# Expert results of a graph and mixture layer added into the output tensor itself, with the copy from a scratch tensor left out

## The reference, cut to what matters

```python
xn = _layernorm(x)
x = x + gnn(xn, edges) + linear_attention(xn)      # first residual; the result is called x2 below
x = x + ffn(_layernorm(x))                         # second residual

def ffn(x):                                        # 8 experts, hidden width 384
    gate = x @ Wg + bg
    scores, idx = top_k(gate, 2)                   # two experts for each row
    h = gelu(x @ W1[e] + b1[e])                    # for each expert e
    y = h @ W2[e] + b2[e]
    return sum over the two chosen e of score * y
```

## Time and profile before

| what | value |
|---|---|
| median of three runs | 1122.59 us |
| the profiled execution's own time | 1124.31 us |
| its span, first to last instruction | 1122.6 us |
| mean granted clock of TensorE | 0.932 of full speed |
| PE busy | 977.9 us, 87% of the span |
| DVE busy | 760.7 us, 68% |
| ACT busy | 332.5 us, 30% |
| POOL busy | 117.2 us, 10% |
| DMA queue of SyncE and ScalarE plain transfers (q1) | 49514 packets, 116.25 MB |
| DMA queue of GpSimd's indirect transfers (q0) | 6048 packets, 21.24 MB |

### The profile page before, as it was taken

The page is one execution under the profiler, slowest core; times in us unless marked ns, Lnnn a source line. Parts: engine busy times, 40 slices in busy tenths (PEclk is TensorE's granted clock), DMA queues, the critical chain, the costliest instruction groups (busy, mean ns, idle before and its releaser), DMA issues.

```text
span 1122.6 us, 17243 instructions
## 1 busy us (share of the span) xinstructions
PE 977.9 (87%) x6460; PEld 708.2 (63%) x6460; DVE 760.7 (68%) x1704; ACT 332.5 (30%) x402; POOL 117.2 (10%) x123
## 2 busy tenths in 40 slices
PE   3799999999789979989988988969887399999991
PEld 2677776765454445545678988858865366666660
DVE  6576788877875686986587898599979823332221
ACT  3561122112004332522333333215335232222220
POOL 3000000000001000000000000000631123333321
PEclk9789999999989999999989999969898599999996
DMA  7350121134341826637687100006056545556546
GB/s 237 105 167 29 57 86 58 57 128 176 107 178 35 297 87 233 185 101 251 225 318 298 47 1 1 1 0 254 5 186 227 209 103 102 109 112 113 110 59 166
DMA packets 58521, 146.44 MB, mean 130 GB/s; under 512 B 11386, under 2 KB 30732, under 8 KB 55434
## 3 DMA queue, kind: packets, MB, share of 16 engines
q1 hardware_dynamic: 49514, 116.25, 29.6%
q0 software_dynamic: 6048, 21.24, 10.0%
q10 hardware_dynamic: 2880, 7.87, 1.8%
HBM read 95.94 MB, written 53.23 MB: 133 GB/s over the span
## 4 chain that ended last, share of the span: by engine, by line
PE 66%; DVE 21%; issue 4%; DMA 4%; ACT 3%; SPq 1%; DVEq 0%; POOLq 0%; ACTq 0%
PE PS L1733 39%; PE PS L1982 12%; DVE arena L1449 3%; PE PS L1809 3%; DVE arena L1455 3%; DVE arena L1493 3%; PE PS L2133 2%; PE PS L1789 1%; PE PS L1820 1%; PE PS L1824 1%; DVE arena L1465 1%; DMA arena<-in_L_gnn_W_dram 1%; DVE arena L1355 1%; DVE arena L1205 1%; DMA arena<-as_d 1%
## 5 line engine op out<-in xcount | busy, mean ns | idle before, releaser
L1733 PE MATMUL PS<-arena 128*128 128x384 f16 (+7 forms) x3396 | 573.0, 322 | 4.6 <-DVE arena L1719 1.9
L1733 PEld LDWEIGHTS PS<-arena 128*128 128x128 f16 (+2 forms) x3396 | 321.0, 99 | 214.8 <-issue 12.2
L1982 PE MATMUL PS<-arena 128*128 128x193 f32 (+1 forms) x1200 | 191.3, 323 | 21.7 <-DVE arena L1455 16.3
L1982 PEld LDWEIGHTS PS<-arena 128*128 128x128 f32 x1200 | 186.7, 200 | 26.3 <-DVE arena L1455 16.0
L1020 ACT ACTIVATE arena<-arena,AS 128x1280 f32<-128x1280 f32 x60 | 81.8, 1363 | 134.0 <-DVE arena L1449 133.8
L1723 DVE TENSOR_SCALAR arena<-PS,arena 128x768 f32<-128x768 f32 x27 | 27.5, 1018 | 138.1 <-PE PS L2159 138.1
L1449 DVE SCALAR_TENSOR_TENSOR arena<-arena,AS 128x1280 f32<-128x1280 f32 x60 | 94.4, 1576 | 0.0
L1455 DVE SCALAR_TENSOR_TENSOR arena<-arena 128x1280 f32<-128x1280 f32 x60 | 90.8, 1513 | 2.5 <-PE PS L1982 2.4
L1257 DVE TENSOR_SCALAR arena<-arena 128x240 f16<-128x240 f16 x324 | 90.0, 278 | 0.0
L1256 DVE TENSOR_SCALAR arena<-arena 128x128 f16<-128x128 f16 x324 | 81.1, 250 | 0.1
L1087 ACT ACTIVATE arena<-PS 128x1536 f16<-128x1536 f16 x27 | 39.2, 1451 | 100.3 <-PE PS L2133 100.3
(11 more groups left out here) (274 smaller groups left out, 953.1 us busy)
## 6 DMA issues: line engine op xcount, KB each, us to landing
arena<-in_L_ffn_W_dram SPq DMA_DIRECT2D x48, 384.0 KB, 4.1
fr_d<-arena SPq DMA_DIRECT2D x48, 384.0 KB, 3.3
arena<-fr_d SPq DMA_DIRECT2D x16, 1152.0 KB, 14.4
arena<-in_x_dram SPq DMA_DIRECT2D x18, 384.0 KB, 5.7
arena<-rr_d SPq DMA_DIRECT2D x4, 1280.0 KB, 8.3
acc_d<-arena SPq DMA_DIRECT2D x11, 384.0 KB, 2.6
g_d<-arena SPq DMA_DIRECT2D x10, 388.0 KB, 2.3
acc_d<-arena ACTq DMA_DIRECT2D x10, 384.0 KB, 2.3
```

What stands on the lines that cost most here:

```text
L1733: m = T.matmul(out, left[i][x], right[i][y], start=first and i + r == 0, stop=last and 3 * i + r == n - 1)
L1982: m = T.matmul(ps[b][:, r * (C + 1):(r + 1) * (C + 1)], PT[i % deep][:, d * P:(d + 1) * P], feats, start=t == 0 and r == 0, stop=t == NT - ...
```

## The change

The stores of x2 go to the output tensor `out` in place of `acc_d`, and the indirect adds go to `out` too. The last tile's store writes its 98 real rows only. The adds get a bound, N - 1 = 1249: an index above it is left out and is no error. So the results of empty slots (numbers from 1280 on) and of the 30 padding rows (1250 to 1279) are written nowhere. The final DMA from `acc_d` to `out` and the wait on it are gone, as are the tile of zeros written to the end of `acc_d` and its share in two waits. `acc_d` still carries the sums of the first residual.

```diff
@@ line 292
-        acc_d = nc.dram_tensor("acc_d", (NP + P, D), F32, kind="Internal").ap()
+        acc_d = nc.dram_tensor("acc_d", (NP, D), F32, kind="Internal").ap()
@@ SyncE, line 583
-            sp.dma_start(acc_d[NP:NP + P, :], zrow).then_inc(s_xs_blank, 16)
@@ SyncE, the end, line 739
-            sp.dma_start(out, acc_d[0:N, :]).then_inc(s_out_done, 16)
-            sp.wait_ge(s_out_done, 16)
@@ GpSimd, line 847
-            pool.wait_ge(s_xs_blank, 32)
+            pool.wait_ge(s_xs_blank, 16)
@@ GpSimd, sums_add, line 858
-                g.indirect_dma_start(out=acc_d, out_offset=bass.IndirectOffsetOnAxis(ap=found[:, i:i + 1].bitcast(U32), axis=0),
-                                     in_=Yb[:, i % 2, :], in_offset=None, compute_op=ALU.add).then_inc(sums_out[i % 2], 16)
+                g.indirect_dma_start(out=out, out_offset=bass.IndirectOffsetOnAxis(ap=found[:, i:i + 1].bitcast(U32), axis=0),
+                                     in_=Yb[:, i % 2, :], in_offset=None, compute_op=ALU.add, bounds_check=N - 1, oob_is_err=False).then_inc(sums_out[i % 2], 16)
@@ ScalarE, line 972
-            act.wait_ge(s_xs_blank, 32)
+            act.wait_ge(s_xs_blank, 16)
@@ ScalarE, sum_out, line 1052
-                a.dma_start(acc_d[t * P:(t + 1) * P, :], X[:, t, :]).then_inc(s_x2_out, 16)
+                r = LAST if t == NT - 1 else P
+                a.dma_start(out[t * P:t * P + r, :], X[0:r, t, :]).then_inc(s_x2_out, 16)
```

More of the change, by code:

```diff
@@ L502, in gps_layer @@
         s_y_ready = sem("y_ready")
-        s_out_done = sem("out_done")
         DENSE = 6 * NT
```

## The result

| | before | changed |
|---|---|---|
| first comparison, median (runs) | 1124.64 us (4) | 1111.95 us (4) |
| second comparison, median (runs) | 1123.67 us (11) | 1108.31 us (6) |
| profiled execution, time and span | 1124.31, 1122.6 | 1116.81, 1115.1 |
| second profile of each, span | 1123.4 | 1109.7 |
| first add of the loop, in the two profiles | 913.53, 914.37 | 920.04, 914.72 |

The ratio of changed to before is 0.9889 in the first comparison (95% interval 0.9848 to 0.9929) and 0.9863 in the second (0.9823 to 0.9904). I had predicted 1106, range 1102 to 1111; the first median is 0.95 us above the range, the second lies inside it. The runs of both kernels spread by 10 us and more over the two comparisons, and the last two rows of the table show where it lies: in the profiles all of it is ahead of the expert loop.

A forecast was written before the change was run, and what follows sets the result against it. It took TensorE to bound the expert loop and the bare final copy the end. Gains of 14.0 (copy), 0.46 (earlier start) and 2.25 us (last add's data) made 16.7, off a median of 1122.59: 1106 us, range 1102 to 1111.

The forecast's parts named there:

- What bounds the kernel, and the loop: End: copy bare, no engine busy; expert loop: TensorE bounds at 7.35 us a tile, adds in its shadow.
- three signs by which I would have known myself wrong: Last add landing 5 us after start; add issue far from 1.59 us; TensorE idle before products awaiting a gather or `Yb`.
- the signs for being right: Among them: copy gone, last add at about 1102.4, span end 1105 to 1106.5, 900 to 1000 fewer packets, 7.35 us tiles.
- The copy, 14.0 us: At the end: removing the copy leaves the last add as last event, closing 0.43 us behind it; gain 14.0 us.
- Rows left out, 2.25 + 0.46: Last add: out-of-bounds rows get no transfer, saving 2.25 us of data; it also starts 0.46 us sooner.
- The test of the bound, nothing: Issue of the adds on GpSimd: testing the bound was taken to make no difference to issue time.
- both rivals about issue time: Adds in the loop: longer issue, most gain kept (1113.8 us, chance 0.06); add chain becomes the bound (about 1147, 0.04).
- The packets: GpSimd's queue: 900 to 1000 fewer packets, from 3456 slots less 2500 real ones.
- The stores of x2 and the tile of zeros, nothing: Ahead of the loop: stores land 42 us early; the zeros' removal gains 0, bounds 0 and 0.47 us.
- The sum: Whole kernel: 14.0 for the copy, 0.46 for the earlier start, 2.25 for the last add's data: 16.7 us.
- the copy alone: Rival at the end: rows left out of the result but not the work; only 14.0 us gained, 1108.5; chance 0.28.

The follow-up runs named there:

- the bound alone: Kernel before with the bound on its adds and nothing else, the copy kept: 1121.47 us against 1124.92, ratio 0.9976.
- empty tiles passed over: Changed kernel with the 26th and 27th slot tile under a condition, skipped if they hold no row: 1099.94 us, ratio 0.9776 against the kernel before.

## Why the prediction was wrong, step by step

**What bounds the kernel, and the loop.** Right. The copy was bare, the adds run in TensorE's shadow, a tile takes 7.35 us in both kernels, TensorE has no gap from 913 to 1060. None of the three signs by which I would have known myself wrong appeared: the last add landed in 2.7 us and not 5, its issue time stayed, and TensorE kept its 147.00 busy us of 147.00. Of the signs for being right, the end of the span (1105 to 1106.5) and the packets failed.

**The copy, 14.0 us.** Wrong in one term, and this is the step that failed: "so 0.43 us of closing follows" and "the closing of 0.43 us the span would end at 1108.56". I took the closing behind the copy for the closing behind any last event. In the kernel before, GpSimd's DRAIN had run out 12 us before the end, so those 0.43 us are the closing with everybody else waiting. Behind the last add of the changed kernel it is 3.6 us (landing at 1111.5, end at 1115.1), because GpSimd's DRAIN runs until 1114.83. The experiment with only the copy out puts the copy at 11.7 us.

**Rows left out, 2.25 + 0.46.** The mechanism was right: nothing moves for them, the last two adds land in 2.7 us (3.05 predicted, 1.15 us after the issue where I took 1.5), and the last add starts 188.75 us after the first instead of 189.30 (188.84 forecast). The page of the Trainium skill that I had weighed against it, "DMA: Bandwidth & Descriptors", section "Anatomy of one DMA — SWDGE (gpsimd) path", gives about 2.0 us of fixed cost, setup and completion together. Here an empty add takes 2.7 us from its start and 1.15 us after its issue, so on neither count 2.0, and the measurement decides. It landed 0.35 us sooner than I had said, and none of that reached the end, because the end of the DRAIN keeps its distance from the issue (4.5 us) and not from the landing.

**The test of the bound, nothing.** Right: 1586 ns before and after, so both rivals about issue time fall.

**The packets.** Wrong. I expected 900 to 1000 fewer; there are as many, and the bytes fell. The adds of empty tiles still show 144 packets each, with 0.00 MB in them.

**The stores of x2 and the tile of zeros, nothing.** No effect was seen. My reading of the cover was careless, though: VectorE waits for all five loads of that group (L1262), and the last of them, b2, is issued at 62.06 us and lands 6.8 us later, at 68.9. The cover was 2.8 us, not 5.2.

**The sum.** From the first add on, 14.0 us measured against 16.7. Counted from the landing, the closing is 3.2 us longer than I had it (3.6 against 0.43); the landing came 0.44 us sooner (0.35 by the landing time, 0.09 by the start). That leaves 2.7 us, which moves the forecast of 1106 to 1108.7. The rest of the way to 1111.95, 3.3 us, I put on the stray ahead of the loop and not on the change, since the traces show the change's own part from the first add on. Of this 2.05 are the kernel before itself, whose median in the same comparison was 1124.64, that much above the one I built on; the changed kernel's four runs lie between 1109.4 and 1116.8. The stray in the traces comes from ahead of the loop, most of it between the last store of the attention sums and the first tile of x2: 265.0 us in one profile of the kernel before and 268.7 in the first of the changed one, but also 268.7 with only the copy out and 265.0 with the last add left out. What makes it the one or the other I haven't found.

**The rival that came nearest** was the copy alone, 14.0 us and 1108.5. That its size is that of the measured 14.0 is luck, for its reason is wrong: the rows left out do come out of the work, and the drain happened to eat about as much (3.2 us) as they gave (2.7 as forecast and 0.4 more).

## What to carry to other kernels

A last event that is removed uncovers all that ran beneath it, the closing instructions of the block included: before costing it, list every engine's last instruction and its DRAIN, and take the latest of them as the new end. Let the engine with the longest closing finish first; here that is GpSimd, and one needless add at its end cost 5.4 us. Compare traces from an event next to the change, not from the start, when the part ahead of it strays by as much as the change is worth.

## What the runs showed of the hardware that I had not expected

GpSimd's DRAIN at the end of the program is long, and two things bound its end from below. In no trace did it end earlier than 4.4 us after the issue of the last add was through (4.5 in the changed kernel, 4.5 with the bound alone, 4.4 without the last add), and it was 4.48 us long where all had landed at its start. Where a transfer with data was still under way it ended about 2 us after the landing (before 2.3, copy alone 2.2, empty tiles passed over about 2). What it does in that time no row tells. In the changed kernel the DRAINs of the others took 0.01 (SyncE), 0.5 (ScalarE), 1.1 (VectorE) and 2.0 us (TensorE).

An indirect add with every row out of bounds still sends 144 packets, all under 512 bytes, and still completes its semaphore, 2.7 us after its start.
